# Causal attention: score blocks of the diagonal packed into full-width exponentials, with a new timetable

## What is computed

```python
q_lat, k_lat, v_lat = [(xn @ W).reshape(b, t, 16, 64) for W in (Wq_down, Wk_down, Wv_down)]
q = concat([q_lat @ Wq_up_c, rope(q_lat @ Wq_up_e)])      # k in the same way, v = v_lat @ Wv_up
scores = einsum('bhqd,bhkd->bhqk', q, k) / 4, masked causally with -inf
y = einsum('bhqk,bhkd->bhqd', softmax(scores), v)
out = x + y @ Wc + feed_forward(xn)                       # xn: layer norm of x
```

## Time and profile before

| | |
|---|---|
| runs of the kernel before, median | 1970.04 us (1965.76 to 1972.16) |
| the profiled execution's own time | 1966.68 us |
| its span, first to last instruction | 1964.9 us |
| PE busy | 1860.7 us, 95% of the span |
| DVE busy | 1697.8 us, 86% |
| ACT busy | 1611.4 us, 82% |
| POOL busy | 554.1 us, 28% |

### The profile page before, as it was taken

The page is one execution under the profiler, slowest core; times in us unless marked ns, Lnnn a source line. Parts: engine busy times, 40 slices in busy tenths (PEclk is TensorE's granted clock), DMA queues, the critical chain, the costliest instruction groups (busy, mean ns, idle before and its releaser), DMA issues.

```text
span 1964.9 us, 42229 instructions
## 1 busy us (share of the span) xinstructions
PE 1860.7 (95%) x13881; PEld 694.6 (35%) x13881; DVE 1697.8 (86%) x4770; ACT 1611.4 (82%) x2108; POOL 554.1 (28%) x712
## 2 busy tenths in 40 slices
PE   6899999999789999999999999999999999999998
PEld 6455565555322222222232322223232222223223
DVE  5699999999888898989899998989999899989861
ACT  2467666765269999999999999999999999999994
POOL 0112111221313424241442424143242414334211
PEclk8899999999769999999999999999999999999999
DMA  4133323335421404042341414133131414314012
GB/s 172 35 92 101 104 82 89 101 101 110 108 66 29 65 21 63 21 62 37 62 65 42 62 43 83 34 65 63 44 62 40 83 29 73 59 43 67 29 36 81
DMA packets 160327, 129.04 MB, mean 66 GB/s; under 512 B 95344, under 2 KB 144752, under 8 KB 159768
## 3 DMA queue, kind: packets, MB, share of 16 engines
q1 hardware_dynamic: 160152, 126.88, 30.0%
HBM read 74.60 MB, written 42.98 MB: 60 GB/s over the span
## 4 chain that ended last, share of the span: by engine, by line
PE 48%; ACT 16%; DVE 3%; issue 3%; DMA 2%; SPq 2%; POOL 1%; ACTq 0%; POOLq 0%; DVEq 0%
PE pv L1511 20%; ACT prob L1304 12%; PE st L1498 11%; PE sm L1477 10%; PE sm L1448 3%; ACT excess L1297 3%; PE st L1486 3%; DMA scratch_i<-inverse 1%; DVE pm L1383 1%; DVE sm L1379 1%; PE sm L1472 1%; SPq L913 1%; DVE sm L1368 0%; ACT Y L1287 0%; DMA Yc<-Y 0%
## 5 line engine op out<-in xcount | busy, mean ns | idle before, releaser
L1304 ACT ACTIVATE prob<-st 128x1024 f32<-128x1024 f32 (+3 forms) x1280 | 1078.3, 900 | 77.8 <-PE st L1498 66.1
L1511 PE MATMUL pv<-prob,V 128*32 128x512 f32 (+3 forms) x5120 | 594.1, 541 | 0.4 <-POOL prob L1261 0.2
L1368 DVE CUSTOM_DVE_ANT_0 sm<-sm,mask 128x128 f32<-128x128 f32 (+3 forms) x1024 | 491.6, 510 | 62.5 <-PE sm L1477 50.3
L1477 PE MATMUL sm<-K,Q 48*128 48x512 f16 (+3 forms) x2112 | 522.7, 349 | 16.3 <-DVE pm L1383 4.3
L1498 PE MATMUL st<-Q,K 50*128 50x512 f16 (+3 forms) x2560 | 484.1, 353 | 28.5 <-ACT prob L1304 21.1
L1261 POOL TENSOR_SCALAR_AFFINE_SELECT prob<-prob 128x256 f32<-128x256 f32 x512 | 206.1, 409 | 932.3 <-ACT prob L1304 926.5
L1383 DVE TENSOR_REDUCE pm<-sm 128x1 f32<-128x512 f32 x640 | 416.8, 683 | 24.3 <-PE sm L1477 22.1
L1379 DVE CUSTOM_DVE_ANT_0 sm<-sm,excess 128x512 f32<-128x512 f32 x448 | 311.1, 716 | 33.7 <-PE sm L1477 25.8
L1477 PEld LDWEIGHTS sm<-K,Q 48*128 48x128 f16 x2112 | 167.5, 94 | 324.9 <-DVE pm L1383 158.6
L1498 PEld LDWEIGHTS st<-Q,K 50*128 50x128 f16 x2560 | 126.6, 93 | 421.3 <-ACT prob L1304 299.6
L1297 ACT ACTIVATE excess<-st 128x1024 f32<-128x1024 f32 x219 | 224.8, 1026 | 17.6 <-PE st L1486 10.8
(11 more groups left out here) (171 smaller groups left out, 1939.0 us busy)
## 6 DMA issues: line engine op xcount, KB each, us to landing
Q<-scratch_q SPq DMA_DIRECT2D x102, 128.0 KB, 4.5
K<-scratch_k SPq DMA_DIRECT2D x102, 128.0 KB, 7.2
x<-in_x SPq DMA_DIRECT2D x16, 512.0 KB, 4.4
scratch_v<-Rt SPq DMA_DIRECT2D x64, 128.0 KB, 2.0
scratch_r<-Rt SPq DMA_DIRECT2D x16, 512.0 KB, 3.2
V_raw<-scratch_v SPq DMA_DIRECT2D x16, 512.0 KB, 10.1
Yc<-Y SPq DMA_DIRECT2D x124, 64.0 KB
spread<-scratch_i SPq DMA_DIRECT2D x124, 64.0 KB, 2.2
```

The lines of the kernel that those rows point to most:

```text
L1304: act.activation(prob[(slot * UNITS + k) % PT][:, :, 0:width], st[number % ST][:, :, 0:width], ACT.Exp)\
L1368: dve.tensor_tensor_reduce(x, x, mask[:, CH - width:], 1.0, -3e38, ALU.add, ALU.max, pm[:, row, t, k:k + 1]).then_inc(sm_read, 1)
L1477: pe.matmul(dst[:, 0:block_width(t, k)], lhsT=Q[slot][r, h // 2, t * P:(t + 1) * P], rhs=K[slot][r, h // 2, k * CH:k * CH + block_width(t, ...
L1511: i = pe.matmul(pv[2 * DH * h:2 * DH * (h + 1), CH - width:CH], lhsT=V[quad % VSLOTS][:, j, h, :], rhs=prob[(slot * UNITS + 2 * n + h // 2 ...
```

## The change

The diagonal blocks of a chunk (widths 512, 384, 256, 128 for each of two pairs of heads, eight units) become five units, each of which fills its two banks: two of 512; two "mixed" units with the 384 and the 128 wide block side by side; one "shared" unit with the 256 wide blocks of both pairs of heads. Every exponential is then 2 x 512 wide, and a quad has 68 units instead of 80. The steps of weighted sums become 36 instead of 40: the blocks of 384 and 128 are one step with twice the matmuls. The matmuls are as many, and as wide, as before. Masks: the shared unit has one instruction over its four blocks, the mixed ones two each, 28 a quad instead of 32. A mixed or shared unit issues both its blocks on one half of the rows and then both on the other. The edge blocks of the maxima stay one to a bank. `TIMETABLE` is new (257 letters: 139 m, 14 x, 68 s, 36 w), `AHEAD` is 70, and the four `project` entries stand up to two places earlier.

```diff
-PROJECT_AT = (78, 91, 107, 121)
+PROJECT_AT = (76, 91, 105, 119)
-AHEAD = 73
+AHEAD = 70
-ORDER = [(c, j, CH - P * max(0, j - SUB * c)) for c in range(TC) for j in range(SUB * (c + 1))]
+def score_units():
+    units, steps = [], []
+    for c in range(TC):
+        wide = [j for j in range(SUB * c + 1)]
+        for j in wide:
+            first = len(units)
+            units += [(c, ((hp, j, CH, 0),)) for hp in range(G // 2)]
+            steps.append((c, ((j, CH, ((first, 0), (first + 1, 0))),)))
+        d, first = SUB * c, len(units)
+        units += [(c, ((hp, d + 1, 3 * P, 0), (hp, d + 3, P, 3 * P))) for hp in range(G // 2)]
+        steps.append((c, ((d + 1, 3 * P, ((first, 0), (first + 1, 0))), (d + 3, P, ((first, 3 * P), (first + 1, 3 * P))))))
+        units.append((c, ((0, d + 2, 2 * P, 0), (1, d + 2, 2 * P, 2 * P))))
+        steps.append((c, ((d + 2, 2 * P, ((first + 2, 0), (first + 2, 2 * P))),)))
+    return units, steps
...
 TIMETABLE = (
...
+    "mwxmmsmwsmmxmmxmmsmmswmxmsmwmxmmswsmmwsmsmmmsmmmmssmwmmsmsmxmmwxmmsm"
+    "msmmswxmmsmwmmsmswmsmwmssmmwmmxmsmwxmmmswmmssmwmsmmswmsmmsmswmxmmxmm"
+    "msmmmsmsmwsmmmswmsmsmwsmmmswmsmmsmwmsmsmmwmsmsmmwmsmmsmwsmsmmwsmsmmw"
+    "xmmmswsmmswmmswsmmsmwmsmmsmwxmmsmwmsmmsmwmsmsmmwmsmms"
...
+            def diagonal_blocks(quad, n, u):
+                x = prob_of(quad, u)
+                at = DIAGONAL_AT[n]
+                if len(UNITS_OF[n]) == 1:
+                    return [(x[:, :, :].rearrange("p g (k q) -> p (g k) q", k=len(at))[:, :, 0:P], 2 * len(at))]
+                return [(x[:, :, a:a + P], 2) for a in at]
...
-                        act.activation(prob[(slot * UNITS + k) % PT][:, :, 0:width], st[number % ST][:, :, 0:width], ACT.Exp)\
-                            .then_inc(exp_done, 1)
+                        act.activation(prob_of(quad, k)[:, :, :], st[number % ST][:, :, :], ACT.Exp).then_inc(exp_done, 1)
...
                 for a in both_halves():
                     r = slice(ROW * a, ROW * a + KD + 2)
-                    i = pe.matmul(st[number % ST][:, a, 0:width], lhsT=K[slot][r, u % 2, j * P:(j + 1) * P],
-                                  rhs=Q[slot][r, u % 2, (c + 1) * CH - width:(c + 1) * CH], start=True, stop=True)
+                    for hp, j, width, at in parts:
+                        i = pe.matmul(st[number % ST][:, a, at:at + width], lhsT=K[slot][r, hp, j * P:(j + 1) * P],
+                                      rhs=Q[slot][r, hp, (c + 1) * CH - width:(c + 1) * CH], start=True, stop=True)
                 i.then_inc(st_ready, 1)
...
-                if diag[n]:
-                    pe.wait_ge(masked, quad * DIAG + 2 * sum(diag[:n + 1]))
+                if DIAGONAL[n]:
+                    pe.wait_ge(masked, quad * sum(MASKS) + sum(MASKS[:n + 1]))
...
+                for j, width, src in blocks:
+                    for h in range(G):
+                        u, at = src[h // 2]
+                        i = pe.matmul(pv[2 * DH * h:2 * DH * (h + 1), CH - width:CH], lhsT=V[quad % VSLOTS][:, j, h, :],
+                                      rhs=prob_of(quad, u)[:, h % 2, at:at + width],
+                                      start=n == STEP_AT[c], stop=n + 1 == STEP_AT[c + 1], tile_position=(0, 2 * DH * h))
+                i.then_inc(pair_used, 1)
```

More of the change, by code:

```diff
@@ L763 @@
 VSLOTS = 2
-UNITS = sum(2 * G * (c + 1) for c in range(TC))
-PAIRS = UNITS // 2
-DIAG = 2 * SUB * TC
 GROUPS = ((0, 1), (2,), (3,))
@@ L896 @@
 UNITS_RUN = len(NUMBERS[0])
[L897 removed]
+assert UNITS_RUN % ST == 0 and SLOTS * NE % SM == 0 and SLOTS * NX % EXCESSES == 0
 LOADS = 4 * len(QROWS)
@@ L997, in attention, with prob_of @@
         I_v = scr["I"].rearrange("k h t -> k (h t)")
-        order = ORDER
-        diag = [j >= SUB * c for c, j, _ in order]
+        def prob_of(quad, u):
+            return prob[(quad * UNITS + u) % PT]
         def unit_done(quad, number):
@@ L1241, in body @@
-                for n, (c, j, width) in enumerate(order):
-                    if last and n == SUB * (TC - 1) * TC // 2 + SUB:
+                for n in range(STEPS):
+                    if last and n == STEP_AT[TC - 1] + SUB:
                         normalise_late(0)
-                    if last and n == sum(SUB * c for c in range(1, TC + 1)) - SUB:
+                    if last and n == STEP_AT[TC - 1] + SUB * (TC - 1):
                         normalise_late(1)
-                    if n == SUB * (TC - 1) * TC // 2 and quad and quad % 2 == 0:
+                    if n == STEP_AT[TC - 1] and quad and quad % 2 == 0:
@@ L1247, in body @@
                         normalise(quad - 1, 1)
-                    if n == SUB * (TC - 1) * TC // 2 + (2 if last else SUB + 2) and quad % 2:
+                    if n == STEP_AT[TC - 1] + (2 if last else SUB + 2) and quad % 2:
                         normalise(quad, 0)
-                    if n == SUB * 3 and not last:
+                    if n == STEP_AT[2] and not last:
                         turn, nxt = quad // SLOTS, (slot + 1) % SLOTS
                         difference_of_keys(quad + 1, nxt, (turn + (2 if nxt == 0 else 1)) * (16 * LOADS))
-                    if n == sum(SUB * c for c in range(1, TC)) and not last:
+                    if n == STEP_AT[TC - 1] and not last:
@@ L1264, in body @@
-                assert d == DIAG
+                        for x, count in diagonal_blocks(quad, n, u):
+                            pool.affine_select(out=x, in_=x, compare_op=ALU.is_ge, fill=0.0, base=0,
+                                               pattern=[[0, count], [1, P]], channel_multiplier=-1).then_inc(masked, 1)
             pool.memset(yn[:, :, :], 0.0).then_inc(yn_cleared, 1)
@@ L1282, in evac @@
             def evac(quad, c):
-                ends = sum(x[0] <= c for x in order)
-                act.wait_ge(pair_used, quad * PAIRS + ends + PT // 2)
+                act.wait_ge(pair_used, quad * STEPS + STEP_AT[c + 1])
                 if c % 2 == 0:
@@ L1500, in scores @@
                 i.then_inc(st_ready, 1)
             def weighted_sums(quad, slot, n, last):
-                c, j, width = order[n]
-                if j == 0:
+                c, blocks = STEP[n]
+                if n == STEP_AT[c]:
                     pe.wait_ge(pv_read, quad * TC + c + 1)
-                if diag[n]:
-                    pe.wait_ge(masked, quad * DIAG + 2 * sum(diag[:n + 1]))
-                else:
-                    pe.wait_ge(exp_done, unit_done(quad, NUMBERS[last][2 * n + 1]))
@@ L1510, in weighted_sums @@
-                for h in range(G):
-                    i = pe.matmul(pv[2 * DH * h:2 * DH * (h + 1), CH - width:CH], lhsT=V[quad % VSLOTS][:, j, h, :],
-                                  rhs=prob[(slot * UNITS + 2 * n + h // 2) % PT][:, h % 2, 0:width],
-                                  start=j == 0, stop=j == SUB * (c + 1) - 1, tile_position=(0, 2 * DH * h))
-                    if h == G - 1:
-                        i.then_inc(pair_used, 1)
+                if DIAGONAL[n]:
+                    pe.wait_ge(masked, quad * sum(MASKS) + sum(MASKS[:n + 1]))
+                else:
+                    pe.wait_ge(exp_done, unit_done(quad, NUMBERS[last][UNITS_OF[n][-1]]))
@@ L1547, in _ @@
             quads(body)
-            for n in range(PAIRS - LAG, PAIRS):
+            for n in range(STEPS - LAG, STEPS):
                 weighted_sums(NQ - 1, (NQ - 1) % SLOTS, n, True)
```

106 lines of the change are left out of this document (58 added, 48 removed).

## The result

The changed kernel takes 1957.98 us (median of 9 runs, 1954.66 to 1969.28), the kernel before beside it 1972.16. The ratio is 0.9935, 95% interval 0.9913 to 0.9956: faster by 0.65%, where 1946 us (1.2% under 1970) was forecast. The profiled execution took 1960.21 us, its span is 1958.4, 6.5 us less than the span of before, with a mean granted clock of 0.969 where before had 0.979. (The clock is given as a share of 2.4 GHz: 1.00 is 2.4 GHz throughout, and every record in the attention is at 2.4 or at 1.2 GHz.)

What follows compares the result with a forecast made beforehand. ACT was taken as nearest to a bound, PE's strict order close behind. A quad: -0.76 - 1.15 + 0.3 + 0.1 + 0.1 = -1.4 us; 15.5 quads and the start make -23, giving 1946 us, range 1918 to 1984.

Steps and rivals of the forecast that it cites:

- Term 1: ACT: twelve exponentials fewer a quad over the same elements, 0.063 us fixed cost each, saving 0.76 us a quad.
- Term 2: Diagonal stretches: no narrow exponentials, so no short rounds of `st` between ACT and PE; saves 1.15 us a quad, upper 2.3.
- Term 3: PE: a packed unit's matmuls follow each other on one half of the rows; costs 0.3 us a quad, bounds 0 and 1.7.
- rival F: PE: weight loads not hidden on the same half of the rows; +0.8 us a quad, 1983 us; chance 0.04.
- Term 4: Maxima rows of chunk 3: distance to their first scores falls to 7.6 to 8.6 us, 7.7 needed; costs 0.1 us a quad.
- Term 5: Masks: 28 instead of 32 a quad, mixed sums wait for four; -0.3 to 1.6 us a quad, taken as 0.1 cost.
- Start and last quad: `AHEAD` 70 puts three entries less before the first exponential; -1 us for both, only half the gain in the last quad.
- C: ACT: only the fixed cost of exponentials is saved, 0.4 to 0.9 us a quad, 1956 to 1964 us; chance 0.14.
- E: PE's order becomes the bound, packed units' scores come late; slower, +1.2 us a quad, 1989 us; chance 0.12.
- the rule on weight loads: PE: a weight load overlaps matmuls in flight only when its row group differs, so packed units' second blocks would wait.

Runs made afterwards that it cites:

- the four edits, tail aside: Changed kernel with one step of sums moved three letters, four 128 wide maxima entries widened, full matmuls replacing one-column ones in the first four quads: 1948.4 us, ratio 0.9889.
- the repaired one: Changed kernel with a step of sums moved three letters, 128 wide maxima entries widened, early one-column matmuls replaced by full ones, idle matmuls in the tail: 1947.7 us.

## Why the prediction was wrong, by its own steps

**The frame failed: it took the clock as given.** The prediction read "a granted clock of 2.4 GHz in the attention" from the page and let it stand for the changed kernel. No step, no rival and no bound asked what the new order does to PE's filling: the clock stood in the sum at nothing. In the profiled execution it cost 17.7 us in seven quads and most of the 2.1 us by which the tail grew, and of the 26.4 us that the rest gained 6.5 were left. Yet the timetable was in the diff, and the count of letters between two w (16 against 11) with the narrow entries in between would have pointed to the place. The prediction named the timetable as its weak point at the end ("could move a quad by 1 us either way"), without the mechanism and too small: a fall costs 1.6 to 3.2 us in the quad that has it. The predicted time was 1946 us; with four small edits that keep the clock up, the kernel takes 1947.7. (The prediction's last addition slipped by a microsecond: 1943.7 and 3.4 make 1947.)

**The sum for a quad was right, some terms by cancelling.** Forecast 84.9 us, measured 84.9 without a fall. In its parts:

- Term 1, 0.76 us: ACT's own work fell so (busy 80.38 us a quad after 81.54, 1.2 less, of which a part is the overlap of neighbours); splitting the exponentials again costs 0.4 us of the quad. The term was taken at about twice what it is worth.
- Term 2, 1.15 us, half of an upper 2.3. The diagonal stretches of one undisturbed quad of the changed kernel, in windows:

```profile
991.94:996.16 4.22, 3.95 (x35) 1.19 (x35) 4.11 (x14) 4.22 (x7) 1.54 (x4) 1.00 0.02 8
1009.71:1013.84 4.13, 4.13 (x37) 1.17 (x36) 3.63 (x12) 3.85 (x5) 2.10 (x6) 1.00 1.05 145
1036.66:1039.75 3.09, 3.09 (x31) 0.74 (x23) 3.08 (x10) 2.90 (x4) 1.92 (x5) 1.00 0.04 6
1068.30:1071.77 3.47, 3.47 (x34) 0.98 (x27) 3.39 (x13) 2.96 (x4) 2.08 (x6) 1.00 0.44 113
```

  They last 14.9 us. Their work is 12 wide exponentials, two excess and one copy, 14 x 0.93 + 0.5 = 13.5, so 1.4 us are lost where it was 3.4. The rest of the quad, 70.0 us, holds 68 x 0.93 + 1.5 = 64.7: 5.3 us lost where it was 3.9. The diagonals gave 2.0 us, near the full term, and 1.4 went back elsewhere, 0.6 net. (They last less than the 18.5 us of the forecast also because three of the five excess instructions have left them.) So the reason for halving was wrong: the half that was taken off isn't lost in the diagonals to PE, but 1.4 us are lost in the stretches between them. What makes that loss, the new order, the masks or something else, wasn't separated. The sum came out because terms 3 to 5, taken at 0.5 us together, cost nothing that shows: -1.15 and +0.5 make -0.65, and -0.6 was measured. That is luck in the parts.
- Term 3, 0.3 us: nothing. Alternating the halves changes no undisturbed quad, so the weight loads on the same half add nothing to it either (rival F out).
- Term 4, 0.1 us: nothing, and the distance was sized well. The transpose of that quad starts at 1031.35. SP's last four DMAs, and on PE's timeline the first scores of chunk 3:

```profile
1034.89 2.42 SPq L1095 DMA_DIRECT2D Q<-ml  x4
```

```profile
1039.26 0.39 PE L1547 MATMUL st<-Q,K 50*128 50x512 f16 x2
```

  They end at 1037.31; the first scores of chunk 3 go at 1039.26 with no idle time noted. 7.9 us, within 7.6 to 8.6, and only some 0.2 us to spare with the landing time of the small loads (1.8 us here).
- Term 5, masks, 0.1 us: the other way, and not slightly. Over the whole trace PE's weight loads of the sums waited 30.3 us for masks before and 4.9 after, 1.9 us in the quad of rows 6 and 0.2 in an undisturbed quad of the changed kernel:

```profile
PEld pv L1511 <- POOL prob L1261: 30.3, 80, 0.6
```

```profile
PEld pv L1562 <- POOL prob L1304: 4.9, 17, 1.8
```

  That the sums of a mixed step wait for four masks didn't show. How much of these 1.6 us a quad was on the path, no run tells; it may be a part of what is put down to term 2.
- Start and last quad: first exponential at 560.96 us instead of 561.84, last quad 94.5 instead of 95.3 us from its first exponential to the last. As forecast. The tail, which had no term, grew by 2.1 us, of which 1.7 are the last eight matmuls at half clock (3.65 against 1.99 us).

The books of the profiled execution: 0.9 us at the start, 24.7 in the first 15 quads without their falls (1.4 and more each, as some quads of before took up to 87.5 us), 0.8 in the last, less 17.7 for the falls and 2.1 for the tail: 6.6 us, against 6.5 measured.

**The rivals.** The result lies where C was (1956 to 1964), for another reason. C said that PE waits less and ACT as much, in every quad; but a quad has gained its 1.4 us, and some quads then lose it. E, the only rival about PE's order, thought of the packed units themselves. The Trainium skill has a page that bears on the cause: "TensorE: Matmul & The Clock Gate", section "A second HAM failure mode: psum-queue depth-cycling", tells of a kernel whose clock goes between its two levels because PE pauses briefly between groups of matmuls. The trace agrees in kind: in the stretch shown PE pauses four times, for at most 0.12 us, and the clock falls. Whether the pauses or the narrow blocks bring it, no run here separates. What was weighed ahead of the result from the same page was the rule on weight loads, which changed nothing.

**What stays open.** How thin PE's work must be for a fall wasn't measured. At 46 us, 14 letters without sums brought a fall into twelve quads of the kernel before; 16 letters brought six in one profile of the changed one, three in another, and one with the exponentials split; 13 letters brought one in the four profiles that have them, nine letters (both steps moved) none in one. The letters between them differ, and so does the moment at which a quad comes; why one quad falls and the next with the same letters doesn't is open. An undisturbed quad of 84.9 us without any falls wasn't reached either: the one profile without a fall behind the first quad (the four edits, tail aside) has 85.2.

## What to carry to other kernels

Where PE is near its limit, its clock is a term of the sum: look in windows as short as the work's period for a granted clock under 1.00, and count in an edited order the longest stretch in which PE has only narrow matmuls. A change that takes work or waits from one engine should be read in the undisturbed periods first and then in the others; the two together tell a wrong mechanism from a right one with a side effect. If a fall shows, spread the heavy matmuls before adding idle ones, and keep the move small: one step moved by three letters cost an undisturbed quad 0.2 us and came to 0.9915 of the kernel before, two steps moved by seven and three cost 0.5 us and came to 0.9924, where the changed kernel had 0.9935 and 0.9957.

## What the runs showed of the hardware

- The clock of PE fell to 1.2 GHz in stretches without weighted sums and with pauses of at most 0.12 us (the changed kernel, ahead of 1118.6 us) or 0.5 us (the kernel before with a step moved). Most of these stretches had many matmuls of 128 and 256 columns; the one at 736 us had blocks of 384 and 512. A fall costs 1.6 to 2.2 us in the quads at a clock of 0.98 and 2.7 to 3.2 us in those at 0.96.
- Falls go with the scatter of the runs of one kernel: 14 us in the changed kernel, with mean clocks of 0.959 to 0.970; 11.5 us in the kernel before, with 0.970 to 0.978; 3.3 us in the repaired one, with 0.975 to 0.980.
- One step of sums five letters later cost 33 us in 2000, with the same instructions.
- Idle matmuls don't have to cost time. With two full ones in place of one of a single column, with no other edit, quads 2 and 3 took 84.7 and 84.5 us at full clock, after 85.9 (with a fall) and 84.5 in the run without them. The medians, 1948.4 and 1951.5 us, don't resolve it. Neither profile with these matmuls has a fall in quads 2 and 3; the four profiles with a moved step or split exponentials and without them have one or two each.
